# DLRM tower on one core: eight chunks of two tiles for four of four, lookups from the first tile on, layer 3 with samples stationary

## What is computed

```python
e = jnp.stack([tbl_0[ids[:, 0]], ..., tbl_25[ids[:, 25]]], axis=1)         # 2048 x 26 x 128
sd = jnp.einsum('bfd,bd->bf', e, dense)                                    # 26 products with the dense features
ss = jnp.einsum('bfd,bgd->bfg', e, e)                                      # 325 pairs of tables
z = jnp.concatenate([dense, sd, ss[:, iu, ju]], axis=1)
h = jnp.concatenate([z, dense], axis=1)                                    # 607 wide
h = jnp.maximum(h @ W_top1 + b_top1, 0.0)                                  # 512
h = jnp.maximum(h @ W_top2 + b_top2, 0.0)                                  # 256
y = h @ W_top3                                                             # 1
```

## Time and profile before

| | us |
|---|---|
| median of 3 runs | 392.0 |
| lowest and highest | 391.76, 398.56 |
| the profiled execution | 391.43 |
| its span | 389.6 |

### The profile page before, as it was taken

How to read it: one execution, slowest core, us unless ns; L and a number is a source line. 1 busy time by engine, 2 the same in 40 slices (tenths; PEclk the granted TensorE clock), 3 DMA queues, 4 the chain that set the end, 5 groups by cost and what they waited for, 6 DMA issues and landing times.

```text
span 389.6 us, 12408 instructions
## 1 busy us (share of the span) xinstructions
PE 343.8 (88%) x5434; PEld 262.9 (67%) x5434; DVE 242.3 (62%) x475; ACT 191.2 (49%) x298; POOL 265.4 (68%) x279
## 2 busy tenths in 40 slices
PE   2899985999999997799999987899999988635996
PEld 0566664787788875688788864788788865434873
DVE  0799995587998642688998633488997541102420
ACT  3366665776133328685123258485133158842333
POOL 6777787777777777777777777777777777770000
PEclk9999997899999999999999999899999999958899
DMA  7996113243332214242432214233333212220000
GB/s 193 261 259 168 47 48 102 64 102 93 92 102 87 52 51 96 84 113 84 111 77 88 54 52 120 66 110 82 108 83 88 53 54 57 59 52 16 2 0 0
DMA packets 20090, 33.41 MB, mean 86 GB/s; under 512 B 7908, under 2 KB 10468, under 8 KB 20038
## 3 DMA queue, kind: packets, MB, share of 16 engines
q0 software_dynamic: 8704, 17.84, 18.3%
q1 hardware_dynamic: 11333, 14.78, 13.8%
HBM read 32.60 MB, written 0.01 MB: 84 GB/s over the span
## 4 chain that ended last, share of the span: by engine, by line
PE 71%; POOL 10%; issue 9%; DVE 4%; ACT 3%; DMA 2%; POOLq 0%; SPq 0%; ACTq 0%; DVEq 0%
PE late_bank L462 12%; PE late_bank L534 12%; PE late_bank L463 10%; POOL rows L441 10%; PE gram_bank L501 9%; PE turn_bank L482 6%; PE turn_bank L462 5%; PE turn_bank L463 5%; PE spare_bank L568 2%; PE gram_bank L568 2%; PE spare_bank L634 2%; DVE one_hot L807 2%; ACT turned L325 2%; PE turn_bank L515 2%; DMA rows<-in_tbl_dram,index 2%
## 5 line engine op out<-in xcount | busy, mean ns | idle before, releaser
L441 POOL DMA_INDIRECT rows<-in_tbl_dram,index x272 | 264.5, 973 | 85.1 <-issue 79.8
L809 DVE TENSOR_TENSOR one_hot<-table_ids,row_number 125x512 fp32r<-125x512 int32 x216 | 133.9, 682 | 23.2 <-PE turn_bank L463 15.6
L325 ACT COPY turned<-turn_bank 128x512 f32<-128x512 f32 (+1 forms) x72 | 70.2, 1030 | 36.5 <-PE turn_bank L482 33.2
L462 PE MATMUL late_bank<-one_hot,table_hi 125*128 125x512 f32 x192 | 81.2, 423 | 1.0 <-DVE table_lo L885 1.0
L463 PE MATMUL late_bank<-one_hot,table_lo 125*128 125x512 f32 x192 | 76.6, 399 | 0.0
L501 PE MATMUL gram_bank<-turned 128*27 128x26 f32 x4096 | 55.3, 195 | 15.1 <-issue 14.8
L501 PEld LDWEIGHTS gram_bank<-turned 128*27 128x27 f32 x4096 | 45.9, 109 | 31.6 <-issue 29.4
L482 PE MATMUL turn_bank<-ident,rows 128*128 128x128 f32 x288 | 47.1, 296 | 16.4 <-DMA rows<-in_tbl_dram,index 6.6
L482 PEld LDWEIGHTS turn_bank<-ident,rows 128*128 128x128 f32 x288 | 35.0, 150 | 27.2 <-issue 15.6
L296 DVE COPY gram<-gram_bank 124x208 f32<-124x208 f32 x32 | 12.0, 374 | 65.6 <-PE gram_bank L501 65.5
L462 PEld LDWEIGHTS late_bank<-one_hot,table_hi 125*128 125x128 f32 x192 | 36.6, 191 | 14.6 <-issue 3.8
(11 more groups left out here) (73 smaller groups left out, 338.8 us busy)
## 6 DMA issues: line engine op xcount, KB each, us to landing
table_ids<-in_ids_by_table_dram SPq DMA_DIRECT2D x27, 256.0 KB, 3.2
rows<-in_tbl_dram,index POOLq DMA_INDIRECT x272, 2.7
turned<-in_tbl_dram SPq DMA_DIRECT2D x6, 448.0 KB, 11.8
looked_up<-in_tbl_dram SPq DMA_DIRECT2D x3, 448.0 KB, 5.6
rows<-in_r_dense_features_dram SPq DMA_DIRECT2D x16, 64.0 KB, 3.2
gram<-in_W_top_dram SPq DMA_DIRECT2D x1, 702.0 KB
gram<-in_W_top_dram SPq DMA_DIRECT2D x1, 512.0 KB
turned<-in_tbl_dram SPq DMA_DIRECT2D x6, 52.0 KB
```

The source lines that it names most:

```text
L325: copy(to[:, f0:f1], of).then_inc(rows_copied[n % 2], 1)
L441: pool.indirect_dma_start(out=rows[:, row % RING_ROWS, :], out_offset=None, in_=tables[f], in_offset=bass.IndirectOffsetOnAxis(ap=index[:, ...
L462: pe.matmul(bank, table_hi[:, s, k, :], hot, start=k == 0, stop=False)
L809: last = nc.vector.tensor_tensor(hot, table_ids[0:RK, (c * LOOKUPS + s) % ID_SLOTS, :], row_number[0:RK, k:k + 1].broadcast_to([RK, CHUNK] ...
```

## The change

`SIZES` lists the tiles of each chunk, eight times two, and all counts of semaphores, offsets and widths follow from a `Chunk` (number, first tile, tiles). So each chunk-wide operation (one-hot, lookup, `copy_found`, pairs, layers 1 and 2, relus) is done on 256 columns, twice as often; transposes of products and pairs work on 64 groups for 128. Work that goes by tile stays as it is. `BLOCKS` for chunks of two tiles places 6 blocks after units 1, 2 and 3 of the first tile, and 7, 7, 8 and 8 after those of the second; the first six lookups, but for chunk 0, take three banks in turn. Layer 3 takes 128 samples as stationary operand and one column of weights as moving one; its results stand in a column per tile in `y`, which has a place of its own, and is stored from there while the next chunk runs; the last chunk does it as before. SyncE's list of loads is rearranged to fit. The core of the diff; the rest replaces `c` by `chunk` and `:` by `0:wide`:

```diff
+SIZES = (2, 2, 2, 2, 2, 2, 2, 2)
...
+LATE = 6
+LATE_BLOCKS = {("columns", 6): 4, ("pairs", 2): 4, **{("layer1", n): 4 for n in range(4)}}
 BLOCKS = {
-    **{("unit", t, u): 4 for t in range(1, TILES) for u in range(UNITS)},
-    ("columns", 6): 4, ("pairs", 2): 4,
-    ("layer1", 0): 4, ("layer1", 1): 4, ("layer1", 2): 4, ("layer1", 3): 4,
+    2: {("unit", 0, 1): 6, ("unit", 0, 2): 6, ("unit", 0, 3): 6, ("unit", 1, 0): 7, ("unit", 1, 1): 7,
+        ("unit", 1, 2): 8, ("unit", 1, 3): 8, **LATE_BLOCKS},
+    4: {("unit", 0, 1): 2, ("unit", 0, 2): 3, ("unit", 0, 3): 3, **{("unit", 1, u): 4 for u in range(UNITS)},
+        **{("unit", t, u): 3 for t in (2, 3) for u in range(UNITS)}, **LATE_BLOCKS},
 }
-FIRST_HOTS = ("unit", 0, 2)
...
+def hots_after(chunk, *step):
+
+    blocks = blocks_after(chunk, *step)
+    first = 0 if step == ("unit", 0, 0) else min(blocks.start + HOT_SLOTS, HOTS)
+    return range(first, min(blocks.stop + HOT_SLOTS, HOTS))
...
-        y_bank = late_bank[0][0:1, :]
+        y_bank = late_bank[0][:, 0:TILES]
+        last_y_bank = late_bank[0][0:1, :]
...
+        def copy_products(engine, chunk, n):
 
 
             mine = int(engine is nc.scalar)
             copy = nc.scalar.copy if mine else nc.vector.tensor_copy
 
-            if n // 2 == y_unit // 2:
-
-                engine.wait_ge(stored, (c + 1) * DMA)
-
-            engine.wait_ge(gram_done, c * ALL_UNITS + n + 1)
+            engine.wait_ge(gram_done, chunk.first * UNITS + n + 1)
             of = gram_bank[mine][0:ACROSS, 0:UNIT * LATER].rearrange("p (k f) -> p k f", k=UNIT)
             copy(gram[0:ACROSS, n * UNIT:(n + 1) * UNIT, :], of).then_inc(gram_copied[mine], 1)
...
-            return late_bank[s % 2][:] if s < LATE else whole_turn_bank[(s + 1) % 2]
+        def found_bank(chunk, s):
+
+            if s >= LATE:
+                bank = whole_turn_bank[(s + 1) % 2]
+            elif chunk.n == 0:
+                bank = late_bank[s % 2]
+            else:
+                bank = (spare_bank, *late_bank)[s % 3]
+            return bank[:, 0:width(chunk)]
+
+        def found_before(chunk, s):
+
+
+            return s - (3 if chunk.n > 0 and s < LATE else 2)
 
         def height(k):
...
-            def load_ids(c, s):
-
-                lookup = c * LOOKUPS + s
+            def load_ids(chunk, s):
+
+                lookup = chunk.n * LOOKUPS + s
                 sp.wait_ge(one_hot_made, max(lookup - ID_SLOTS + 1, LOOKUPS) * K_ROWS)
-                sp.dma_start(table_ids[:, lookup % ID_SLOTS, :],
-                             ids_t[LOOKED_UP[s], c * CHUNK:(c + 1) * CHUNK].partition_broadcast(P)).then_inc(ids_loaded[s], DMA)
+                sp.dma_start(table_ids[:, lookup % ID_SLOTS, 0:width(chunk)],
+                             ids_t[LOOKED_UP[s], chunk.first * P:(chunk.first + chunk.tiles) * P].partition_broadcast(P)
+                             ).then_inc(ids_loaded[s], DMA)
...
+            def store(chunk):
+
+                sp.wait_ge(y_copied, chunk.n + 2)
+                sp.dma_start(out[chunk.first * P:(chunk.first + chunk.tiles) * P, :].rearrange("(t p) o -> p (t o)", p=P),
+                             y[:, chunk.first:chunk.first + chunk.tiles], allow_slow_non_contiguous=True).then_inc(stored, DMA)
...
-            for c in range(1, chunks):
-                for s in range(ID_SLOTS):
-                    load_ids(c, s)
-                load_dense(c, 0)
-                load_dense(c, 1)
-                for s in range(ID_SLOTS, LOOKUPS):
-                    load_ids(c, s)
-                load_dense(c, 2)
-                load_dense(c, 3)
-                store(c - 1)
-            store(chunks - 1)
...
+            for chunk in CHUNKS[:-1]:
+
+
+                following, ahead = CHUNKS[chunk.n + 1], chunk.first + RING_TILES
+                load_ids(following, 0)
+                load_ids(following, 1)
+                load_dense(ahead)
+                if chunk.n > 0:
+                    store(CHUNKS[chunk.n - 1])
+                load_ids(following, 2)
+                if chunk.tiles == 2:
+                    load_ids(following, 3)
+                    load_dense(ahead + 1)
+                    load_ids(following, 4)
+                    load_ids(following, 5)
...
-                    hot = one_hot[:, n % HOT_SLOTS, :]
-                    bank = found_bank(s)
+                        wait_all_rows(pe, chunk.first * TURNS)
+                    if k == 0 and found_before(chunk, s) >= 0:
+
+                        pe.wait_ge(found_copied, (chunk.n + 1) * LOOKUPS + found_before(chunk, s) + 1)
+                    if k == 0 and s == 1:
+
+                        pe.wait_ge(y_copied, max(chunk.n, 1))
+
+                    pe.wait_ge(one_hot_made, chunk.n * HOTS + n + 1)
+                    hot = one_hot[:, n % HOT_SLOTS, 0:width(chunk)]
+                    bank = found_bank(chunk, s)
                     pe.matmul(bank, table_hi[:, s, k, :], hot, start=k == 0, stop=False)
                     pe.matmul(bank, table_lo[:, s, k, :], hot, start=False, stop=k == K_ROWS - 1).then_inc(one_hot_used, 1)
...
-                    last = pe.transpose(cols_bank[g][:, i % TURN * P:i % TURN * P + ACROSS], gram[0:ACROSS, :, i],
+                    last = pe.transpose(cols_bank[g][0:high, i % TURN * P:i % TURN * P + ACROSS], gram[0:ACROSS, 0:high, i],
                                         ident[0:ACROSS, 0:ACROSS])
 ...
+                    last = pe.transpose(to[:, q], pairs[0:high, q, k * PK:(k + 1) * PK], ident[0:high, 0:high])
                 last.then_inc(pairs_turned, 1)
...
+                    last = pe.matmul(h1_bank[n][:, 0:wide], w[0:p, k, cols], x[0:p, k, 0:wide],
                                      start=k == 0 and x is input_hi and w is w1_hi, stop=k == K1 - 1 and w is w1_lo)
                 return last
...
+            def layer3(chunk):
+
+                pe.wait_ge(h2_made, (chunk.n + 2) * N2)
+                for t in range(chunk.tiles):
+                    for k in range(N2):
+                        last = pe.matmul(y_bank[:, t:t + 1], h2[:, k, t * P:(t + 1) * P], w3_sb[:, k:k + 1],
+                                         start=k == 0, stop=k == N2 - 1)
+                last.then_inc(y_summed, 1)
...
                     for u in range(UNITS):
-                        if t + 1 < TILES:
-                            turn_rows(c, t + 1, turns_before(u, awaited))
-                        products(c, t, u)
+                        if t + 1 < chunk.tiles:
+                            turn_rows(chunk, t + 1, turns_before(u, awaited))
+                        products(chunk, t, u)
                         if more:
-                            if blocks_before(("unit", t, u)) == 0:
-
-                                pe.wait_ge(y_copied, c + 1)
-                            look_up(c + 1, blocks_after("unit", t, u))
+                            look_up(following, blocks_after(chunk, "unit", t, u))
                     if awaited:
-                        turn_rows(c, t + 1, turns_before(UNITS, awaited))
...
-                        if u == 0 and t == TILES - 2:
-
-                            place_found(act, c, TILES - 1)
+                        if u == 0 and t == chunk.tiles - 2:
+
+                            place_found(act, chunk, chunk.tiles - 1)
                             if more:
-                                copy_found(c + 1, range(blocks_before(("unit", t, 0))))
-                        if t + 1 < TILES:
-                            copy_rows(act, c, t + 1, turns_before(u, awaited))
+                                copy_found(following, range(blocks_before(chunk, ("unit", t, 0))))
+                        if t + 1 < chunk.tiles:
+                            copy_rows(act, chunk, t + 1, turns_before(u, awaited))
                         if u % 2:
-                            copy_products(act, c, t * UNITS + u)
-                        if u == 1 and t < TILES - 2:
-                            place_found(act, c, t + 1)
-                        if more and t >= TILES - 2:
-                            copy_found(c + 1, blocks_after("unit", t, u))
+                            copy_products(act, chunk, t * UNITS + u)
+                        if u == 1 and t < chunk.tiles - 2:
+                            place_found(act, chunk, t + 1)
+                        if more and t >= chunk.tiles - 2:
+                            copy_found(following, blocks_after(chunk, "unit", t, u))
                     if awaited:
-                        copy_rows(act, c, t + 1, turns_before(UNITS, awaited))
+                        copy_rows(act, chunk, t + 1, turns_before(UNITS, awaited))
...
+                    dve.wait_ge(one_hot_used, (chunk.n + 1) * HOTS + n - HOT_SLOTS + 1)
+                    hot = one_hot[:, n % HOT_SLOTS, 0:wide]
+                    if chunk.n == 0:
                         last = nc.vector.tensor_scalar(hot, id_slot(s), row_number_sb[:, k:k + 1], None, ALU.is_equal)
```

(24 more changed lines are left out.)

390 lines of the change are left out of this document (200 added, 190 removed).

## The result

The changed kernel takes **485.88 us** (480.69 to 487.43), against 392.73 for the kernel before in the same comparison: a ratio of 1.236, 95% interval [1.226, 1.246]. Predicted were 415 and a range up to 434. The direction was right, the size was not: 71 us are missing. The profiled execution spans 484.2 us.

The account below looks back on a forecast made before the run. TensorE (85.5 us per four tiles) and GpSimd's gathers (about 85) were taken to run abreast. First products at 54.1, seven chunks of 46.6 and a last of 33 made a 413.3 us span, forecast 415; range 386 to 434.

Parts of the forecast that it names:

- The stores from columns hide behind the next chunk: Layer 3's column stores while the next chunk runs: nothing waits for them until the end, so no cost.
- VectorE hidden: VectorE per new chunk: half-width one-hots at 0.35 us each, 35 of 46.6 us busy, hidden behind TensorE.
- its rival: Second tile's units: half-width one-hots at 0.41 us make VectorE or the identifiers the bound, 436 us; chance 0.09.
- The sum of a chunk: TensorE's terms for two new chunks: 85.5 us plus 7.6 is 93.1, so 46.6 us per new chunk.
- placing: ScalarE places found rows ahead of the row copies; TensorE waits ahead of unit 1, +4.6 us per four tiles.
- transposes, switches, boundary, the 3.3 let go: TensorE, four tiles: product transposes +2.0, pair transposes +1.2, switches +0.5, chunk boundary +2.0, tile 0's instruction gap -3.3 us.
- Preparation: Nine tables before the chunks: 3.6 us each with one-hots at 0.28, first products at 54.1 for 66.84.
- Last chunk: Final chunk of two tiles: 14.5 us before the layers and 18.3 from there on, 33 in all.
- The matmul of 256 columns: TensorE's lookups and layers 1 and 2: 0.118 us each, ends 0.107 and 0.156; +0.6 us per four tiles.
- GpSimd would wait and not bind: Gathers need 42.6 us per new chunk against 46.6, so GpSimd waits some 4 us per chunk for turned rows.
- The half clock after a wait: Chunk boundaries: TensorE's clock falls after waits, up to 1.7 us per stretch, 427 us; chance 0.07.
- the third: Third sign that the prediction is wrong: VectorE has no idle time in the second tile.

Follow-up runs that it names:

- f2: Changed kernel with layer 3 and every chunk's store as in the kernel before (a row of 256, one contiguous store); 441.8 us.
- g2: f4 with a ring of eight one-hot slots of 256 columns for four of 512; 413.5 us.
- f4: f2 with the found rows placed behind the row copies and unit 1's product copy, as in the kernel before; 423.6 us.
- h1: Changed kernel without the stores of the first seven chunks, layer 3 still making columns; 439.3 us.
- g1: Changed kernel with its column stores cut to the first of each chunk's two columns, 128 elements for 256; 473.8 us.
- f3: Kernel before with only layer 3 and the store changed: results in columns, the first three chunks stored from them; ratio 1.040.
- h3: Changed kernel with each column store issued behind the last of a chunk's loads of identifiers, in the second tile; 441.9 us.
- h7: f3 with its first two column stores moved behind the chunk's identifiers and the third behind the last products; 390.6 us.
- e4: Same edit as f3 on the kernel before, run on a slow chip where the kernel before took 677.66 us; 676.9 us.

## Why the prediction was wrong

**The step that failed**: "The stores from columns hide behind the next chunk, as nothing waits for them until the end", with which the change cost 0 there. f2 against the changed kernel puts it at 43.3 us, of the 71 missing. I asked only who waits for the store, and not what it does to the others on the same DMA engines, nor what those others carry. No row of before held such a store, and I gave no bound above nothing for it, against my own rule for what isn't shown. What it does in the first tile: the packets of gathers and of instructions take up to 6.2 and 3.4 us, TensorE stands, and its signals to the other engines come up to 8.5 us late.

**Steps that were mis-sized.**
- *VectorE hidden.* The one-hot of half width was right (0.351 us each, 176.9/504, for 0.35), and its rival asked for 0.41 before VectorE could bind. But what counts is the ring, not the mean: four slots of half width hold half the work, and a unit takes up to eight. g2 puts that at 10.1 us.
- *The sum of a chunk.* Rid of the store, the placing and the ring, g2's chunk is 46.3, where the prediction had 46.6 with 2.3 for placing, so 44.3 without: 2.0 us, 14 in all. Over two chunks TensorE is busy 2 x 43.58 = 87.2, against the 80.50 + 4.3 that my terms make, and idle 5.4 against 3.7. Which of my small terms (transposes, switches, boundary, the 3.3 let go) is short wasn't tried. The last isn't gone: f4 has 0.78 for instructions in the first tile even with lookups around.
- *Preparation.* 3.75 us for a table in the middle of it, for 3.6: one-hots were 0.33 and not 0.28 each. First products at 56.4 for 54.1.
- *Last chunk.* 38.8 for 33. f2 has 34.0, which puts the seventh store, which meets products without lookups, at 4.8; h1, without any store there, has 36.6, which puts it at 2.2.

In all 43 (stores, 4.8 of it in the last chunk by f2) + 10 (ring) + 14 (chunk) + 2 (preparation) + 1 (last chunk) = 70 of the 71. Chunks after f4 and g2:

```profile
198.18:246.98 48.80, 45.52 (x808) 40.73 (x807) 35.53 (x104) 21.26 (x49) 32.23 (x35) 1.00 0.30 76
```

```profile
193.00:239.30 46.30, 43.58 (x809) 39.30 (x806) 34.94 (x104) 21.01 (x49) 32.52 (x35) 1.00 0.33 80
```

**Steps that held.** The matmul of 256 columns, the term that carried the sum, in the changed kernel:

```profile
177.85 0.28 PE L521 MATMUL late_bank<-one_hot,table_hi 125*128 125x256 f32 x1
177.97 0.28 PE L522 MATMUL late_bank<-one_hot,table_lo 125*128 125x256 f32 x1
178.09 0.28 PE L521 MATMUL late_bank<-one_hot,table_hi 125*128 125x256 f32 x1
```

They start 0.12 apart, and twelve of layer 1 take 1.41, 0.1175 each, for 0.118. By the formula of the Trainium skill (TensorE: Matmul & The Clock Gate, Back-to-back issue gap), which leaves out the loading of weights, it would be 0.109; with new weights for each matmul the rows are above it here as they were at 512 columns. Placing cost its 2.3 per chunk. That GpSimd would wait and not bind was right; it waits 74 us, more than double the 4 us per chunk that I named. The half clock after a wait, given 0.07, is real in five chunks of seven; what it costs came on the term for placing, whose size was right in part by luck, as the wait alone saves 1.07 in chunk 3.

Of the ways in which I said that it could be wrong, the third came in part: VectorE sets the pace within the second tile's units. The direction came from the terms for small matmuls, waits and boundaries. As a sum they stand, to within 2 us a chunk on the low side, but they weren't tried one by one: without the stores' 43 us the kernel is still 12% slower, and without placing and ring too (g2) 5%.

## What to carry to other kernels

A transfer that nobody waits for isn't free: ask what shares the DMA engines with it while it runs, packets of instructions included, and put it where the engines need few instructions. Where a wait has no releaser that the profile can name, look at when the semaphore rose, and who raises it. Where a width is halved, a ring counted in pieces holds half the work; count it against the longest burst, not against the mean. And for an operation that no row shows, keep an upper end in the range, however harmless it looks.

## What the runs showed of the hardware

- Behind a store of 256 or 512 single floats from 128 partitions the DMA engines are 70% to 98% busy at 33 to 44 GB/s for some 3 to 9 us, in all four kernels shown. In the changed kernel the store's own packets are not what fills them (9 ns each); packets of gathers take up to 6.2 us each, against 1.5 in f2. 16 floats do nothing to the time (438.8 against 439.3 us without a store), 128 most of it (g1).
- Packets of instructions share the DMA engines and come slow or late there too: they take up to 3.4 us in the changed kernel for 1.7 in f2, and in f3 one started 8.3 us behind a chunk's first products for 2.7 in the kernel before.
- What it costs depends on where it falls: some 6 us where TensorE runs 72 or more small matmuls in 3 us (5.76 us of waiting for instructions in f3), little or nothing where it runs 14 to 28 (h3, h7). In the changed kernel some of TensorE's signals to VectorE and ScalarE rise 2.6 to 8.5 us after the matmul is recorded as ended (up to 8.1 in f3), where f2, h1, h3, h7 and the kernel before have 0.6 at most. "Remote" in the changed kernel is thus TensorE itself.
- That the slow packets of instructions are the whole cause fits all runs, but no run changes them alone: some waits end up to 10.7 us behind the start of the slow packet (285.0 and 274.3). Why a store of small pieces slows the packets of others stays open.
- After a wait of 2.02 us TensorE's clock was at the lower of its two levels while twelve 256-column matmuls ran at 0.21 us, and so in five of f2's seven chunks with such a wait; gaps of 0.26 and 0.78 left it at full speed in the same chunk of f4.
- The same chip had the kernel before at 677.7 us in one set and at 391.8 in a later one. e4, which took 676.9 in the first, has 165 us of waits there for nothing that the profile names.
